# Graph network on one core: edge features of the gather stage scaled on ScalarE, second linear maps applied after the segment sums

## The reference, cut to what matters

```python
outA = wA * g0 * e0
outB = wB * jnp.einsum('euk,ek->eu', g1, e1) / SQRT3
outC = (wC * g0)[..., None] * e1[:, None, :]
outD = wD[..., None] * g1 * e0[..., None]
mA, mB, mC, mD = (seg(outA) * inv, seg(outB) * inv, seg(outC) * inv, seg(outD) * inv)
c0 = (mA @ W_l2_A0 + mB @ W_l2_B0) * s
c1 = (einsum(mC, W_l2_C1) + einsum(mD, W_l2_D1)) * s[..., None]
angle = 0.1 * (mA @ W_l3_A + mB @ W_l3_B) * s
return cos(angle) * merge(sc0, sc1) + sin(angle) * merge(c0, c1)
```

## Time and profile before

| | |
|---|---|
| median of 3 runs | 5270.04 us |
| lowest, highest | 5262.52, 5271.84 us |
| span of the profiled execution | 6176.2 us |
| profiled execution, time outside its span | not given |
| busy, share of the span: PE, PEld | 60%, 49% |
| DVE, ACT, POOL | 47%, 45%, 66% |
| mean granted TensorE clock | 0.695 of full speed |

### The profile page before, as it was taken

How to read it: one execution, slowest core, us unless ns; L and a number is a source line. 1 busy time by engine, 2 the same in 40 slices (tenths; PEclk the granted TensorE clock), 3 DMA queues, 4 the chain that set the end, 5 groups by cost and what they waited for, 6 DMA issues and landing times. The chain is left out here.

```text
span 6176.2 us, 86140 instructions
## 1 busy us (share of the span) xinstructions
PE 3676.8 (60%) x18515; PEld 3020.3 (49%) x18515; DVE 2879.2 (47%) x12091; ACT 2789.4 (45%) x9367; POOL 4072.2 (66%) x3270
## 2 busy tenths in 40 slices
PE   5555555555555555555474667665676666676666
PEld 3333434434333443433254566655565656666655
DVE  6565565556556555655471233333333333333334
ACT  2222222222222222222264567665665766676666
POOL 4888888888888888888745455544554545555552
PEclk7766666666776666667686666677666677766676
DMA  8666666666666666666772222222222222222221
GB/s 275 110 114 114 111 112 116 111 111 115 112 111 112 116 111 111 115 111 108 143 209 66 53 67 63 60 62 56 62 66 58 64 59 64 66 64 59 65 61 43
DMA packets 703023, 587.38 MB, mean 95 GB/s; under 512 B 287194, under 2 KB 572431, under 8 KB 701430
## 3 DMA queue, kind: packets, MB, share of 16 engines
q0 software_dynamic: 285872, 224.40, 26.2%
q1 hardware_dynamic: 394090, 297.48, 17.4%
q10 hardware_dynamic: 23004, 64.87, 2.8%
HBM read 374.12 MB, written 212.29 MB: 95 GB/s over the span
## 5 line engine op out<-in xcount | busy, mean ns | idle before, releaser
L786 POOL DMA_INDIRECT sums_scratch<-vals,to_i x1564 | 2455.1, 1570 | 543.9 <-issue 361.4
L1115 POOL DMA_INDIRECT fg<-f_scratch,src_e x1564 | 1482.7, 948 | 1389.5 <-DMA src_e<-in_src 757.2
L1179 ACT ACTIVATE hot<-raw,e_s 128x40 f32<-128x40 f32 x6272 | 1447.7, 315 | 436.1 <-issue 339.4
L704 PE MATMUL ps_n<-same,hot 128*40 128x128 f32 x3136 | 695.5, 415 | 1317.7 <-issue 1314.7
L704 PEld LDWEIGHTS ps_n<-same,hot 128*40 128x40 f32 x3136 | 556.7, 184 | 1426.8 <-issue 1362.5
L1144 PE MATMUL ps_eu<-hot,prod 128*128 128x120 f32 x3136 | 901.8, 373 | 280.6 <-issue 279.6
L1305 DVE TENSOR_TENSOR prod<-ps_ew,fg 128x256 f32<-128x256 f32 x392 | 164.3, 419 | 1711.0 <-remote 1304.4
L1142 PE MATMUL ps_eu<-hot,prod 128*128 128x40 f32 x3136 | 619.5, 280 | 429.3 <-issue 410.5
L1142 PEld LDWEIGHTS ps_eu<-hot,prod 128*128 128x128 f32 x3136 | 635.6, 242 | 481.0 <-issue 468.8
L1144 PEld LDWEIGHTS ps_eu<-hot,prod 128*128 128x128 f32 x3136 | 627.3, 243 | 299.0 <-issue 298.7
L744 ACT COPY near<-ps_n 40x512 f32<-40x512 f32 x196 | 113.3, 578 | 1420.7 <-PE ps_n L704 931.6
(11 more groups left out here) (210 smaller groups left out, 4269.3 us busy)
## 6 DMA issues: line engine op xcount, KB each, us to landing
srow_s<-in_src SPq DMA_DIRECT2D x194, 512.0 KB
hid_scratch<-hid SPq DMA_DIRECT2D x196, 256.0 KB
hid_e<-hid_scratch SPq DMA_DIRECT2D x196, 256.0 KB
e_s<-in_edge_attr SPq DMA_DIRECT2D x194, 256.0 KB
sums_scratch<-zeros ACTq DMA_DIRECT2D x12, 2112.0 KB, 30.5
sums_scratch<-vals,to_i POOLq DMA_INDIRECT x1564
fg<-f_scratch,src_e POOLq DMA_INDIRECT x1564
t_in<-sums_scratch POOLq DMA_DIRECT2D x72, 256.0 KB, 8.1
```

Source lines behind the costliest of these rows:

```text
L704: last = pe.matmul(ps_n[t // TH][:, t % TH, :], hot[:, k, t, :], same[:, k, t, :], start=True, stop=True)
L786: pool.indirect_dma_start(out=sums_d[i], out_offset=bass.IndirectOffsetOnAxis(ap=to_i[:, j, t:t + 1], axis=0), in_=vals[:, j, t, :], in_of ...
L1115: pool.indirect_dma_start(out=fg[:, j, t, :], out_offset=None, in_=f_d, in_offset=bass.IndirectOffsetOnAxis(ap=src_s[:, j, t:t + 1], axis= ...
L1179: last = act.activation(hot[:, k, t, c, :], raw[:, k, t, :], ACT.Copy, scale=e4_s[:, j, t, c:c + 1])
```

## The change

`hot` shrinks to one product with the first edge attribute, 8 ACTIVATEs of 40 elements a group. The other three attributes, the directions, are no longer multiplied into the one-hot matrix: ACT multiplies them into the gathered features (`scaled`), for each of 8 tiles three ACTIVATEs that take 32 scalar features and 32 of one vector component, so 24 of 64 elements a group, after a wait for the gathers. DVE makes the first half of `prod` as before, then waits for `scaled`, sums the three components over the directions (`dot`, a reduction of 768 elements to 256), and multiplies weights into the second half (one product of 768, one of 256 elements).

On PE the product of 120 columns becomes one of 40 against `raw`. The linear maps and the copies out of PSUM ahead of them are gone from the groups: DVE adds `ps_eu` straight into the table, one step earlier (group s-2), and the maps are applied to each finished half block in four products of 129 columns with the angle as the 129th, in place of the transposes. The copies of the transposed values on DVE are gone with them. SP now waits for `e_scaled` and `e_prod` of group s-4 in place of `e_hot` and `e_fc2`. DVE waits for the segment sums of s-2 ahead of `raw`. Four fewer weight loads are made late in the scatter stage.

```diff
@@ -584,21 +584,16 @@
                       ALU.add).then_inc(s_res, 1)
 def late_weights():
-    dve.wait_ge(w_in, 16 * 24)
-    for d in range(3):
-        c = MUL * (d + 1)
-        dve.tensor_scalar(lin_f[c:c + MUL, d + 1, 0:MUL], lin_f[c:c + MUL, d + 1, 0:MUL],
-                          3.0 ** -0.5, None, ALU.mult)
-        dve.tensor_scalar(ang_f[c:c + MUL, 0:1], ang_f[c:c + MUL, 0:1],
-                          3.0 ** -0.5, None, ALU.mult)
+    dve.wait_ge(w_in, 16 * LATE)
+    dve.tensor_scalar(lin_f[3 * MUL:D, 1, :], lin_f[3 * MUL:D, 1, :], 3.0 ** -0.5, None, ALU.mult)
     dve.tensor_scalar(fc2_w[:, :], fc2_w[:, :], 1.0 / 8.0, None, ALU.mult).then_inc(w_scaled, 1)
     dve.wait_ge(w_scaled, 1)
     dve.tensor_copy(node_w[:, 0:MUL], sc_f[:, 0:MUL])
     dve.tensor_copy(node_w[:, MUL:D].rearrange("p (w d) -> p d w", d=3),
                     sc_f[:, MUL:D].rearrange("p (d w) -> p d w", d=3))
-    dve.tensor_copy(lin_w[:, 4, :], ang_f[:, 0:1].to_broadcast([P, D]))
-    dve.tensor_copy(lin_w[:, 0:4, 0:MUL], lin_f[:, :, 0:MUL])
-    dve.tensor_copy(lin_w[:, 0:4, MUL:D].rearrange("p k (w d) -> p k d w", d=3),
+    dve.tensor_copy(lin_w[:, :, 0:MUL], lin_f[:, :, 0:MUL])
+    dve.tensor_copy(lin_w[:, :, D:D + 1], lin_f[:, :, D:D + 1])
+    dve.tensor_copy(lin_w[:, :, MUL:D].rearrange("p k (w d) -> p k d w", d=3),
                     lin_f[:, :, MUL:D].rearrange("p k (d w) -> p k d w", d=3))
...
 raw = tmp("raw", [P, 2, TS, W])
-hot = tmp("hot1", [P, 2, TS, 4, W])
+hot = tmp("hot1", [P, 2, TS, W])
+scaled = tmp("scaled", [P, 2, TS, 2, 3, MUL])
+dot = tmp("dot", [P, TS, MUL])
 prod = tmp("prod", [P, 2, TS, 2, D])
-sums = tmp("sums", [P, 2, 2, 4, W])
-sums_a = tmp("sums_a", [P, 2, 2, W])
 ps_w = [bank(f"ps_ew{i}", [P, TS, 4, MUL], s4) for i in range(2)]
-ps_u = [bank(f"ps_eu{i}", [P, 2, 4, W], s4) for i in range(2)]
-ps_cb = [bank(f"ps_ec{i}", [P, 512], s4) for i in range(2)]
-ps_c = [ps_cb[i][:, 0:4 * W].rearrange("p (g h w) -> p g h w", g=2, h=2) for i in range(2)]
-ps_lin = ps_cb[0][:, 4 * W:4 * W + HB].rearrange("p (c d) -> p c d", c=HC)
-ps_ang = ps_cb[0][:, 4 * W + HB:4 * W + HB + HC]
-assert HB == HC * D
+ps_u = [bank(f"ps_eu{i}", [P, 2, 2, W], s4) for i in range(2)]
+ps_lin = bank("ps_lin", [NP, HC, D + 1], s4)
...
@@ -1096,8 +1086,8 @@
     e0 = first_edge(sp, s)
     uses(sp, gath[j], q, 16 * TS)
     settle(sp, passed)
-    done(sp, e_hot, s, UN)
-    done(sp, e_fc2, s, UN)
+    done(sp, e_scaled, s, UN)
+    done(sp, e_prod, s, UN)
...
@@ -1134,36 +1124,24 @@
 m, r, i = at(s, q, j, 1)
 if live_sg(m):
     k = i % 2
+    done(pe, e_hot, m)
     done(pe, e_prod, m)
-    done(pe, e_hot, m)
-    done(pe, e_sums, m, 2)
+    done(pe, e_add, m, 2)
     for t in range(TS):
         hf = t // TH
-        pe.matmul(ps_u[k][:, hf, 0, :], prod[:, k, t, 0, :], hot[:, k, t, 0, :],
+        pe.matmul(ps_u[k][:, hf, 0, :], prod[:, k, t, 0, :], hot[:, k, t, :],
                   start=(t == 0), stop=False, skip_group_check=True)
-        last = pe.matmul(ps_u[k][:, hf, 1:4, :], prod[:, k, t, 1, :], hot[:, k, t, 1:4, :],
+        last = pe.matmul(ps_u[k][:, hf, 1, :], prod[:, k, t, 1, :], raw[:, k, t, :],
                          start=False, stop=(t == TS - 1), skip_group_check=True)
     last.then_inc(e_seg, 1)
-m, r, i = at(s, q, j, 2)
 if j == 2 and live_self(q - 2):
     done(pe, g_stage, q - 2)
-    done(pe, e_add, m if live_sg(m) else NSG + i, 2)
-    done(pe, g_lin, q - 2, 1)
+    done(pe, g_y, q - 2, 1)
     for c in range(HC):
-        pe.transpose(ps_lin[:, c, :], staged[:, 0, c:HB:HC], ident[:, :])
-    for c in range(HC):
-        last = pe.transpose(ps_ang[:, c:c + 1], staged[0:1, 1, c:HB:HC], ident[0:1, 0:1])
+        for g in range(2):
+            last = pe.matmul(ps_lin[:, c, :], staged[:, g, c:HB:HC], lin_w[:, g, :],
+                             start=(g == 0), stop=(g == 1))
     last.then_inc(g_tr, 1)
-if live_sg(m):
-    k = i % 2
-    done(pe, e_sums, m)
-    done(pe, e_add, m, 2)
-    if j == 0 and live_self(q - 3):
-        done(pe, g_lin, q - 3)
-    for c in range(4):
-        pe.matmul(ps_c[k][:, 0, :, :], lin_w[:, c, :], sums[:, k, :, c, :], start=(c == 0), stop=(c == 3))
-    last = pe.matmul(ps_c[k][:, 1, :, :], lin_w[:, 4, :], sums_a[:, k, :, :], start=True, stop=True)
-    last.then_inc(e_lin, 1)
 sweep(pe, body, 0, END, FIRST, 192)
@@ -1175,17 +1153,20 @@
     done(act, e_raw, s)
     done(act, e_seg, s, 2)
     for t in range(TS):
-        for c in range(4):
-            last = act.activation(hot[:, k, t, c, :], raw[:, k, t, :], ACT.Copy,
-                                  scale=e4_s[:, j, t, c:c + 1])
+        last = act.activation(hot[:, k, t, :], raw[:, k, t, :], ACT.Copy,
+                              scale=e4_s[:, j, t, 0:1])
     last.then_inc(e_hot, 1)
-m, r, i = at(s, q, j, 1)
-if live_sg(m):
-    done(act, e_seg, m)
-    done(act, e_lin, m, 2)
-    for c in range(4):
-        act.copy(sums_a[MUL * c:MUL * (c + 1), i % 2, :, :], ps_u[i % 2][MUL * c:MUL * (c + 1), :, c, :])
-    act.copy(sums[:, i % 2, :, :, :], ps_u[i % 2][:, :, :, :]).then_inc(e_sums, 1)
+    if idle_tiles(s):
+        act.wait_ge(gath[j], 16 * (TS * (q + 1) - IDLE))
+    else:
+        uses(act, gath[j], q + 1, 16 * TS)
+    done(act, e_prod, s, 2)
+    for t in range(TS):
+        of_t = fg[:, j, t, :].rearrange("p (g u) -> p g u", g=4)
+        for d in range(3):
+            last = act.activation(scaled[:, k, t, :, d, :], of_t[:, 0:d + 2:d + 1, :], ACT.Copy,
+                                  scale=e4_s[:, j, t, d + 1:d + 2])
+    last.then_inc(e_scaled, 1)
 if j == 0 and live_self(q - 4):
     hb = q - 4
@@ -1216,20 +1197,14 @@
 @block.vector
 def _(dve):
-def from_sums(hb):
-    done(dve, g_tr, hb)
-    done(dve, g_y, hb, 1)
-    dve.tensor_copy(lin[:, :, :], ps_lin[:, :, :])
-    done(dve, g_trig, hb, 1)
-    dve.tensor_scalar(th[:, :], ps_ang[:, :], 0.1, None, ALU.mult).then_inc(g_lin, 1)
 def angle(hb):
     def link(i, ins):
         ins.then_inc(g_th, 1)
         dve.wait_ge(g_th, hb * ANGLE + i)
-    done(dve, g_lin, hb)
+    done(dve, g_tr, hb)
+    done(dve, g_trig, hb, 1)
     at_h = attr_h[:, bass.ds(hb * HC, HC)]
-    link(1, dve.scalar_tensor_tensor(out=th[:, :], in0=th[:, :], scalar=1.0 / 32.0, in1=at_h,
+    link(1, dve.scalar_tensor_tensor(out=th[:, :], in0=ps_lin[:, :, D], scalar=0.1 / 32.0, in1=at_h,
                                      op0=ALU.mult, op1=ALU.mult))
     link(2, dve.tensor_scalar(k2[:, :], th[:, :], 0.15915494309189535, ROUND, ALU.mult, ALU.add))
@@ -1259,7 +1234,7 @@
     settle(dve, passed)
     done(dve, g_o, hb, 1)
     for c in range(HC):
-        last = dve.scalar_tensor_tensor(out=y[:, c, :], in0=lin[:, c, :],
+        last = dve.scalar_tensor_tensor(out=y[:, c, :], in0=ps_lin[:, c, 0:D],
                                         scalar=sin_a[:, c:c + 1], in1=t_sb[:, c, :],
                                         op0=ALU.mult, op1=ALU.add)
@@ -1293,36 +1268,41 @@
                       ALU.subtract).then_inc(e_rel, 1)
     done(dve, e_rel, s)
     done(dve, e_hot, s, 2)
+    done(dve, e_seg, s, 2)
     dve.tensor_tensor(raw[:, k, :, :], iota_f[:, None, 0:W].to_broadcast([P, TS, W]),
                       rel[:, :, :].rearrange("p h k -> p (h k)")[:, :, None].to_broadcast([P, TS, W]),
                       ALU.is_equal).then_inc(e_raw, 1)
-    done(dve, e_fc2, s)
+m, r, i = at(s, q, j, 2)
+if live_sg(m):
+    b0 = dve.value_load(base_i[0:1, bass.ds(m * 2, 1)], min_val=0, max_val=N)
+    b1 = dve.value_load(base_i[0:1, bass.ds(m * 2 + 1, 1)], min_val=0, max_val=N)
+    done(dve, e_seg, m)
+    done(dve, e_add, m, 1)
+    to = table[:, :, bass.ds(b0, W)]
+    dve.tensor_tensor(to, ps_u[i % 2][:, 0, :, :], to, ALU.add).then_inc(e_add1, 1)
+    done(dve, e_add1, m)
+    to = table[:, :, bass.ds(b1, W)]
+    dve.tensor_tensor(to, ps_u[i % 2][:, 1, :, :], to, ALU.add).then_inc(e_add, 1)
+if live_sg(s):
     if idle_tiles(s):
         dve.wait_ge(gath[j], 16 * (TS * (q + 1) - IDLE))
     else:
         uses(dve, gath[j], q + 1, 16 * TS)
-    for g in range(2):
-        dve.tensor_tensor(prod[:, k, :, g, 0:MUL], ps_w[k][:, :, g, :], fg[:, j, :, 0:MUL], ALU.mult)
-        last = dve.tensor_tensor(
-            prod[:, k, :, g, MUL:D].rearrange("p t (d u) -> p t d u", d=3),
-            ps_w[k][:, :, 2 + g, None, :].to_broadcast([P, TS, 3, MUL]),
-            fg[:, j, :, MUL:D].rearrange("p t (d u) -> p t d u", d=3), ALU.mult)
-    last.then_inc(e_prod, 1)
-m, r, i = at(s, q, j, 3)
-if live_sg(m):
-    b0 = dve.value_load(base_i[0:1, bass.ds(m * 2, 1)], min_val=0, max_val=N)
-    b1 = dve.value_load(base_i[0:1, bass.ds(m * 2 + 1, 1)], min_val=0, max_val=N)
-    done(dve, e_lin, m)
-    if j == 3 and live_self(q - 2):
-        from_sums(q - 2)
-    done(dve, e_add, m, 1)
-    to = table[:, :, bass.ds(b0, W)]
-    dve.tensor_tensor(to, ps_c[i % 2][:, :, 0, :], to, ALU.add).then_inc(e_add1, 1)
-    done(dve, e_add1, m)
-    to = table[:, :, bass.ds(b1, W)]
```

(44 more changed lines are left out.)

1 line of the change is left out of this document (removed).

## The result

The changed kernel takes **5688.8 us** (median of 4 runs, 5687.5 to 5690.4) against 5270.5 for the kernel before in the same comparison (4 runs): a ratio of 1.080, 95% interval 1.078 to 1.081, slower. The forecast was 5668 us.

The account below looks back on a forecast made before the run. POOL's gathers, 10.0 us a group, were taken as the bound, to be replaced by a DVE-ACT ring of 12.26. Groups end at 5662, less 16 is 5646, with tail 5691, against the median 5703, less 34 rounded 5668 us; range 5545 to 5850.

Parts of the forecast that it names:

- The ring: Gather stage: `raw`, `hot`, `scaled`, `dot`, products, next `raw`, closed by program order through DVE and ACT, 12.26 us a group.
- End-of-layer parts lose their cover: DVE's angle, normalisation, table copy and combination, formerly covered by POOL's 10 us, now lie in the ring: 1.60 us a group.
- the end of a turn of the loop: Idle time ahead of `rel` and a later `raw`: 0.54 us for four groups, 0.14 a group in the ring.
- PE's relief brings nothing: Removed matmuls save no time, since PE stands in no ring and its work was within 9.8 us a group.
- POOL idles 2.3 us a group and is never late: Gather stage: gathers 10.0 and landing 1.6 us fit the ring's lead, even with a 30 us load of indices.
- The sum: First products' end at 3270.8, 2391 us of ring, end parts, tail and corrections, rounded to 5668 us.
- The tail: From the end of the last products to the end of the span: 48 us less 3 saved.
- the 34 us taken off for it: Half of the up to 68 us by which the scatter stage may end earlier than in the trace.
- the 906 us of unexplained time: The profiled span of 6176.2 us over the median of 5270.0, placed in the gather stage as stretch of the profiled execution.
- 10.0 to 10.4 us a group with POOL as the bound: Undisturbed gather stage of the kernel before: POOL's 8 gathers at 1.25 us, 10.0 us a group, as the bound.
- Rival 2: PE and ACT bound the undisturbed gather stage at 12.5 us a group; the ring replaces that, 5230 us; chance 0.05.
- Rivals 1 and 3: 1: dearer copies or `dot`, together up to 6172 us, chance 0.12; 3: POOL remains the bound, 5267 us, chance 0.04.

Follow-up runs that it names:

- The wait in the old kernel: The kernel before with one added wait, DVE for `hot` of the same group ahead of the products: 6311.8 us against 6128.1, ratio 1.029.
- the longer ring: The changed kernel with 18 more unused copies a group on ACT behind the 24: 6614.6 us; with DVE's end-of-layer parts moved ahead of the wait for `scaled`, 6383.4.

## Why the prediction was right, point by point

- **The ring and its length: right.** Forecast 12.26 us a group, measured 12.21. That it is closed by program order, not by work, is shown twice by kernels that run the same instructions and differ in the order of two blocks (and in which of the two SP waits for). The wait in the old kernel points the same way, but there the other bound is mixed in.
- **The terms.** The copies start (5.82 - 0.332)/23 = 0.239 apart, by the timeline above and the median length of one (0.332), forecast 0.238. The estimate from the figures of the Trainium skill (ScalarE: Activation LUTs, What ACT_TABLE_LOAD costs), 0.239, agrees with this trace. `dot` takes 0.95 from its start to the next (4530.29 to 4531.24), forecast 0.86. That would be 18 us in all, but the last product takes 0.33 from its start to the next, forecast 0.42, which gives it back. From `scaled` to `dot` 5.85, forecast 5.71 + 0.10 + 0.04. From `dot` to `rel` with the copy out of the table 2.48, forecast 2.49. From `rel` to `hot` 0.72, forecast 0.78, and from `hot` to `scaled` 1.77, forecast 1.75. The turn shown takes 10.82 where the same terms of the forecast give 10.87, as far apart as 12.21 and 12.26.
- **End-of-layer parts lose their cover: right**, 1.60 us a group forecast, and 0.14 for the end of a turn of the loop. The turn above, less the 0.34 of the copy out of the table, is 10.48; to the mean of 12.21 that leaves 1.73. Taking the parts out brought 231 us with the longer ring, 1.2 a group. The rest of the 300 wasn't separated from the other bound.
- **PE's relief brings nothing: right**, the terms of the ring give 12.21 without PE. The profile puts 449 us of PE's waits down to nothing that it shows; in the turn above that wait ends 0.1 us after the last product, which PE needs (4532.10 + 0.42, then 4532.62).
- **POOL idles 2.3 us a group and is never late: right**, 436 us in 196 groups, 2.2. `scaled` waited for a gather once, 8.9 us, when the stage began.
- **The sum.** The products end at 5650.5 (5650.1 + 0.41), forecast 5646: +4. The tail is 37.6 us, forecast 45: -7. Outside the span lie 1.6 us (5689.7 and 5688.1 for the same execution), not 12: -10. The scatter stage did not end earlier, the first gather starts at 3250.5, in the trace before at 3251.3; the 34 us taken off for it were wrong: +34. 5668 + 4 - 7 - 10 + 34 = 5689. So in part it is luck that the sum lies only 21 us off: its errors in the other terms took off 13 of the 34. The length of the ring is no luck: its terms were right within 0.1 us each.
- **What failed: how the profiled execution was read.** The step "since the new kernel has fewer matmuls for the profiler to stretch" took the 906 us of unexplained time for an effect of the profile. The kernel before takes about 6130 in its timed runs too, in three of the four comparisons made after the first, and 6088 in the last. The idle time is there without the profiler. It comes with the gathers: with half of them ACT is busy for 1762 of 1799 us. So 10.0 to 10.4 us a group with POOL as the bound can hold only for the kernel at 5270, of which there is no trace; it fits the median but isn't shown. In the trace of the prediction the bound was something else, 14.6 a group. Rival 2 (0.05) came nearest to this, with a ring of 12.26 against a slower stage before, though with PE and ACT as what bounds it and a profiler that stretches everything. Where the kernel before takes 5270 it fell. Where it is at 6130, the changed kernel isn't slower (1.002), but not faster either, since the other bound holds for it too.
- Rivals 1 and 3 fell: the copies and `dot` had nearly the forecast cost, and with 5.0 us of gathers the changed kernel stayed where it was.
- That DVE would be the cheaper place for the 24 multiplications, as the prediction estimates, was not tried.

What stays open: by which path the gathers hold up the instructions of other engines, and why that happened in all later comparisons and not in the first. The later ones ran on two different chips; on which the first ran isn't known. Two traces of the changed kernel show the difference: at 5689 ACT is never idle inside its blocks of `scaled`, at 6153 it is for 247 us (335 times, 3300 to 6000 us).

## What to carry to other kernels

Before adding a result that one engine makes and another needs in the same group, write down for both engines what stands ahead of what, and follow the arrows round: if they close within one group, the period is at least the sum of the ring, whatever the throughput of each engine, and everything else in it (here 1.6 us of unrelated work) loses its cover. The cure tried here is order, not speed: letting ScalarE make the copies of a group ahead of the part that waits for VectorE was worth 536 us (with 18 more copies) and 732 us (with half of the gathers) with the same instructions. And take a profiled execution far off the median as a sign of another bound until shown otherwise: run the kernel before again beside each experiment, and choose experiments that stand out above whichever bound it shows.
